# Folding the convolution's Fourier transforms round the middle of the sequence in a fused hybrid block

## What is computed

```python
b, l, d = u.shape
up = (u @ w_in + b_in).transpose(0, 2, 1)
uc = lax.conv_general_dilated(up, sf_w[:, None, :], (1,), [(KSIZE - 1, KSIZE - 1)], ...)[..., :l] + sf_b[None, :, None]
x0, x1, v = jnp.split(uc, 3, axis=1)
k = _implicit_filter(...).T
v = v * x1
n = 2 * l
y = jnp.fft.irfft(jnp.fft.rfft(v, n=n) * jnp.fft.rfft(k, n=n), n=n)[..., :l]
v = y + v * filt_bias[None, :, None]
out = (v * x0).transpose(0, 2, 1)
return out @ w_out + b_out
```

## Time and profile before

| what | value |
|---|---|
| median of 3 runs | 515.03 us (514.41 to 516.46) |
| the profiled execution's own time | 516.48 us |
| its span | 514.6 us |
| TensorE busy | 471.2 us (92%) |
| VectorE busy | 364.7 us (71%) |
| GpSimd busy | 327.0 us (64%) |
| ScalarE busy | 270.8 us (53%) |
| TensorE clock granted, mean | 0.981 |

### The profile page before, as it was taken

One profiled execution on the slowest core, in us unless ns is written; L12 is line 12 of the kernel. 1 busy time (PEld: TensorE's weight loads), 2 busy tenths in 40 slices (PEclk: granted clock), 3 DMA queues, 4 the chain that ended last, 5 costly groups with the idle time before them and its releaser, 6 DMA issues.

```text
span 514.6 us, 13024 instructions
## 1 busy us (share of the span) xinstructions
PE 471.2 (92%) x3852; PEld 367.3 (71%) x3852; DVE 364.7 (71%) x1136; ACT 270.8 (53%) x716; POOL 327.0 (64%) x446
## 2 busy tenths in 40 slices
PE   3989999999899999996899999999889999999994
PEld 1658878787665999974576676666677656999962
DVE  6688999967766656544877787878877766566635
ACT  3464444653561555544667676676765542555530
POOL 4455766648772466651798899999746771566640
PEclk9999999998999999999999999999979999999997
DMA  8999950001111233316000000000001111333229
GB/s 280 325 383 406 403 225 1 0 2 41 48 54 47 73 85 95 84 52 165 0 3 3 2 3 2 4 1 3 2 14 36 53 53 47 84 83 95 78 73 291
DMA packets 36993, 47.56 MB, mean 92 GB/s; under 512 B 4186, under 2 KB 28123, under 8 KB 36798
## 3 DMA queue, kind: packets, MB, share of 16 engines
q1 hardware_dynamic: 31648, 35.90, 21.4%
q0 software_dynamic: 4544, 9.35, 5.3%
q10 hardware_dynamic: 734, 1.50, 1.0%
HBM read 17.86 MB, written 28.87 MB: 91 GB/s over the span
## 4 chain that ended last, share of the span: by engine, by line
PE 74%; DVE 10%; ACT 8%; issue 5%; POOL 1%; DMA 0%; ACTq 0%; DVEq 0%; POOLq 0%
PE bank L783 69%; ACT silu_sh L1249 2%; PE bank L305 2%; PE bank L893 2%; DVE prod L1614 2%; ACT rows L1242 1%; ACT scores_odd L1224 1%; ACT wide L1224 1%; DVE conv_xv L1521 1%; ACT k_tok L1224 1%; PE bank L1179 1%; PE bank L795 1%; DVE residual L1620 1%; DVE prod L1791 1%; PE bank L992 1%
## 5 line engine op out<-in xcount | busy, mean ns | idle before, releaser
L660 POOL DMA_INDIRECT routed<-row_out,row_token x78 | 74.9, 960 | 66.4 <-DVE row_token L1682 49.9
L783 PE MATMUL bank<-row_in_t,row_weights 128*128 128x128 f32 x624 | 84.0, 278 | 1.9 <-issue 1.2
L783 PEld LDWEIGHTS bank<-row_in_t,row_weights 128*128 128x128 f32 x624 | 75.7, 192 | 4.2 <-issue 2.8
L651 POOL DMA_INDIRECT sorted_rows<-rows,place x64 | 62.3, 973 | 23.0 <-issue 14.3
L1290 ACT ACTIVATE row_silu<-bank 128x256 f32<-128x256 f32 x78 | 29.9, 383 | 48.2 <-PE bank L783 48.2
L1674 DVE TENSOR_SCALAR row_weights<-experts 128x512 f32 x78 | 33.9, 435 | 26.9 <-issue 23.2
L783 PE MATMUL bank<-wide,weights_sb 128*128 128x512 f32 x112 | 51.5, 597 | 0.0
L783 PE MATMUL bank<-experts,row_act 128*128 x312 | 50.1, 283 | 1.3 <-ACT row_out L1224 1.1
L1249 ACT ACTIVATE silu_sh<-bank 128x512 f32<-128x512 f32 x32 | 19.0, 594 | 60.0 <-PE bank L783 59.8
L1666 DVE TENSOR_TENSOR row_act<-row_silu,bank 128x256 f32<-128x256 f32 x78 | 32.8, 420 | 19.8 <-ACT row_silu L1290 10.9
L1224 ACT ACTIVATE wide<-bank 128x512 f32<-128x512 f32 x54 | 29.4, 592 | 30.8 <-PE bank L783 17.1
(11 more groups left out here) (194 smaller groups left out, 1092.2 us busy)
## 6 DMA issues: line engine op xcount, KB each, us to landing
sorted_rows<-zeros SPq DMA_DIRECT2D x1, 17028.0 KB, 50.6
row_in<-sorted_rows SPq DMA_DIRECT2D x78, 64.5 KB
rows<-routed SPq DMA_DIRECT2D x8, 256.0 KB, 4.9
scores_odd<-routed SPq DMA_DIRECT2D x8, 256.0 KB, 5.3
out<-residual SPq DMA_DIRECT2D x8, 256.0 KB, 3.6
routed<-row_out,row_token POOLq DMA_INDIRECT x78, 2.3
tables_sb<-tables SPq DMA_DIRECT2D x1, 1024.0 KB, 8.8
experts<-rt_gate SPq DMA_DIRECT2D x1, 1024.0 KB, 18.4
```

The costliest lines, as they stand in the source:

```text
L651: pool.indirect_dma_start(sorted_rows, bass.IndirectOffsetOnAxis(ap=place[:, t:t + 1].bitcast(U32), axis=0), rows[:, t, :], None).then_inc ...
L660: pool.indirect_dma_start(routed, bass.IndirectOffsetOnAxis(ap=row_token[:, r:r + 1].bitcast(U32), axis=0), row_out[:, r, :], None).then_i ...
L783: return pe.matmul(out_, lhsT, rhs, start=start, stop=stop, **kw)
```

## The change

The sequence is folded round its middle. Position j and position 255 - j are added into an even half and subtracted into an odd half, 128 positions each. With the transform's origin at the middle, the cosines need the even half alone and the sines the odd half, so `forward` drops the sum over s, and `inverse` makes an even half out of the cosines and an odd half out of the sines. Afterwards the sum of the two is the first half of the sequence, and their difference the second half in reversed order.

- GpSimd `value(k)`: the product as before, then a wait for it, then an addition and a subtraction of 128 x 256 elements, each of which reads half of `value_c` with a step of -1.
- TensorE `forward(k)`: 4 matmuls of 256 columns instead of 8. `inverse(k)`: 8 matmuls of 128 columns instead of 8 of 256.
- ScalarE `copy_odd(k)`: a new copy of the odd half, 256 columns, out of bank 6; it stands behind tap2 in a step. `keep(2)` and `scale_rows(1)` move ahead of copy_odd(7).
- VectorE `gate(k)`: waits for that copy, adds, subtracts (this one writes with a step of -1) into `out_c`, waits for both, and then multiplies `out_c` with `gates`.
- The buffers for it are parts of `scores_odd`, which is idle then. `gate_tap_rows`, `gate_weights` and their semaphores are declared and not used; the short convolution stays as it is. The table that is loaded for the transforms has 1024 columns as before.

```diff
+    centred = np.arange(P)[:, None] - (L - 1) / 2
+    fold_cos, fold_sin = np.cos(2 * np.pi * centred * f / NF), -np.sin(2 * np.pi * centred * f / NF)
+    fold_sin[:, 0] = -np.sin(np.pi * centred[:, 0])
+    fold = np.stack([fold_cos, fold_sin], 1)
+    c["fold_dft"] = fold
+    inv = (fold * weight).transpose(1, 2, 0)
+    c["inverse_dft"] = inv.reshape(2, FB, P, P).transpose(2, 0, 1, 3)
...
             def value(k):
                 pool.wait_ge(c_conv, 3 * k + 2)
+                pool.tensor_tensor(value_c[:], conv_xv[:, 0, :], conv_xv[:, 1, :], ALU.mult).then_inc(c_value, 1)
+                pool.wait_ge(c_value, k + 1)
                 wait(pool, c_value_turned, k)
-                pool.tensor_tensor(value_c[:], conv_xv[:, 0, :], conv_xv[:, 1, :], ALU.mult).then_inc(c_value, 1)
+                v = value_c[:].rearrange("p (b t) -> p b t", b=2)
+                folded = value_fold.rearrange("p (b h t) -> p b h t", b=2, h=2)
+                for h, op in enumerate((ALU.add, ALU.subtract)):
+                    pool.tensor_tensor(folded[:, :, h, :], v[:, :, 0:P], v[:, :, L - 1:P - 1:-1], op).then_inc(c_folded, 1)
...
             def forward(k):
                 pe.wait_ge(c_value_copied, k + 1)
                 wait(pe, c_prod, 4 * k)
-                v = value_t[:].rearrange("p (b s) d -> p s b d", s=SB)
+                if k == 0:
+                    pe.wait_ge(inverse_loaded, 16)
+                v = value_t[:].rearrange("p (b h) d -> p h b d", h=2)
                 for c in range(2):
                     for f in range(FB):
                         o = bank[4 + c][:, f * 2 * D:(f + 1) * 2 * D].rearrange("p (b d) -> p b d", b=2)
-                        for s in range(SB):
-                            last = mm(pe, o, dft[:, s, c, f * P:(f + 1) * P], v[:, s, :, :],
-                                      start=(s == 0), stop=(s == SB - 1))
+                        last = mm(pe, o, fold_dft[:, c, f * P:(f + 1) * P], v[:, c, :, :])
...
-                            last = mm(pe, bank[6][:, b * L:(b + 1) * L], y[:, c, f, b, :], inverse_dft[:, c, f, :],
-                                      start=(c == 0 and f == 0), stop=(c == 1 and f == FB - 1))
+                            last = mm(pe, bank[6][:, b * L + c * P:b * L + (c + 1) * P], y[:, c, f, b, :],
+                                      inverse_dft[:, c, f, :], start=(f == 0), stop=(f == FB - 1))
...
+            def copy_odd(k):
+                act.wait_ge(c_inverse, k + 1)
+                copy(act, out_odd, bank[6][:].rearrange("p (b h t) -> p b h t", b=2, h=2)[:, :, 1, :]).then_inc(c_odd_copied, 1)
...
             pipelined([(0, beside({6: second_apply})), (1, each(copy_value)), (1, beside({0: copy_spectrum})),
-                       (2, each(tap2)), (3, each(conv_apply)), (3, each(copy_normed)),
+                       (2, each(tap2)), (0, beside({7: third_keep})), (0, each(copy_odd)), (3, each(conv_apply)),
+                       (3, each(copy_normed)),
                        (0, beside({5: first_apply, 6: third_apply, 7: first_silu}))], PAIRS, 1, first=-1)
...
             def gate(k):
-                dve.wait_ge(c_inverse, k + 1)
+                dve.wait_ge(c_odd_copied, k + 1)
+                even = bank[6][:].rearrange("p (b h t) -> p b h t", b=2, h=2)[:, :, 0, :]
+                y = out_c.rearrange("p (b t) -> p b t", b=2)
+                dve.tensor_tensor(y[:, :, 0:P], even, out_odd, ALU.add).then_inc(c_unfolded, 1)
+                dve.tensor_tensor(y[:, :, L - 1:P - 1:-1], even, out_odd, ALU.subtract).then_inc(c_unfolded, 1)
+                dve.wait_ge(c_unfolded, 2 * (k + 1))
                 wait(dve, c_out, k)
-                dve.tensor_tensor(gated[:], bank[6][:], gates[:, bass.ds(k * PT, PT)], ALU.mult).then_inc(c_gated, 1)
+                dve.tensor_tensor(gated[:], out_c, gates[:, bass.ds(k * PT, PT)], ALU.mult).then_inc(c_gated, 1)
```

More of the change, by code:

```diff
@@ L88 @@
 TABLES, TABLES_N = packed([
-    ("identity", P), ("decay", TAU * D), ("dft", TAU * NF), ("inverse_dft", 2 * FB * L),
+    ("identity", P), ("decay", TAU * D), ("dft", TAU * NF), ("fold_dft", NF), ("inverse_dft", 2 * FB * P),
     ("causal", P), ("own_head", P), ("head_of", HEADS), ("head_in_group", IN_GROUP), ("tie_rank", E),
@@ L113, in shape_constants @@
     weight = np.where(np.arange(NF // 2) == 0, 1.0, 2.0) / NF
-    inv = (dft[:L] * weight).transpose(1, 2, 0)
-    c["inverse_dft"] = inv.reshape(2, FB, P, L).transpose(2, 0, 1, 3)
+    centred = np.arange(P)[:, None] - (L - 1) / 2
[5 more added lines that the diff above has]
+    c["inverse_dft"] = inv.reshape(2, FB, P, P).transpose(2, 0, 1, 3)
     c["identity"] = np.eye(P)
@@ L172, in hybrid_block @@
         dft = table("dft", "p (t c f) -> p t c f", t=TAU, c=2)
+        fold_dft = table("fold_dft", "p (c f) -> p c f", c=2)
         inverse_dft = table("inverse_dft", "p (c f t) -> p c f t", c=2, f=FB)
@@ L320, in hybrid_block @@
         value_c = sb("value_c", [P, PT])
+        scores_odd = sb("scores_odd", [P, 2 * HEADS * P])
+        value_fold = scores_odd[:, 0:PT]
+        out_odd = scores_odd[:, PT:PT + 2 * P].rearrange("p (b t) -> p b t", b=2)
+        out_c = scores_odd[:, 2 * PT:3 * PT]
+        gate_tap_rows = scores_odd[:, 3 * PT:3 * PT + 3 * D]
+        gate_weights = scores_odd[:, 4 * PT:4 * PT + 3 * D].rearrange("p (k d) -> p k d", k=3)
         value_t = sb("value_t", [P, PAIR, D])
@@ L336, in hybrid_block @@
         c_value = sem("c_value")
+        c_folded = sem("c_folded")
+        c_odd_copied = sem("c_odd_copied")
+        c_unfolded = sem("c_unfolded")
+        gate_taps_loaded = sem("gate_taps_loaded")
+        gate_weights_made = sem("gate_weights_made")
         c_value_turned = sem("c_value_turned")
@@ L522, in hybrid_block @@
         v_wide = sb("v_wide", [P, 3, AT, V_N])
-        scores_odd = sb("scores_odd", [P, AT * HEADS * P])
         scores = [s.rearrange("p (t h q) -> p t h q", t=AT, h=HEADS)
@@ L567, in hybrid_block @@
         at_decay, at_dft = slice(*TABLES["decay"]), slice(*TABLES["dft"])
-        at_inverse, at_rest = slice(*TABLES["inverse_dft"]), slice(TABLES["causal"][0], TABLES_N)
+        at_inverse, at_rest = slice(TABLES["fold_dft"][0], TABLES["inverse_dft"][1]), slice(TABLES["causal"][0], TABLES_N)
         conv_columns, other_columns = slice(0, WEIGHTS["w_out"][0]), slice(WEIGHTS["w_out"][0], WEIGHTS_N)
@@ L987, in turn_value @@
             def turn_value(k):
-                pe.wait_ge(c_value, k + 1)
+                pe.wait_ge(c_folded, 2 * (k + 1))
                 pe.wait_ge(ln_c.copied, min(k + 2, PAIRS))
                 for j in range(PAIR):
-                    last = pe.transpose(bank[0][:, j * P:(j + 1) * P], value_c[:, j * P:(j + 1) * P], ident)
+                    last = pe.transpose(bank[0][:, j * P:(j + 1) * P], value_fold[:, j * P:(j + 1) * P], ident)
                 last.then_inc(c_value_turned, 1)
@@ L1388, in third_apply, with third_keep, first_silu @@
                 early_apply(2)
-            def first_silu():
+            def third_keep():
                 keep(2)
                 scale_rows(1)
+            def first_silu():
                 silu_half(0, 0)
```

## The result

The changed kernel takes 518.75 us (median of 19 runs, 516.05 to 523.54); the kernel before, run beside it on the same chip, 516.64 us (19 runs, 514.41 to 517.98). The ratio is 1.0059 (95% interval 1.0042 to 1.0076): 3.0 us slower, just over the 0.5% that this kernel's measurement can tell. Forecast were 516.6 us against 515.03, so +1.6; the range of 511.8 to 521.5 holds the time. By the two medians the change costs 2.1 us and by the two means (519.46 and 516.58) 2.9; where this text says 3.0 it goes by the ratio.

A forecast was written before the change was run, and what follows sets the result against it. TensorE was taken to bound the steps, with VectorE 0.36 us behind. A balance of -0.2 us before the clock plus +1.8 for the clock gave +1.6 on 515.03: 516.6 us, range 511.8 to 521.5.

The forecast's parts named there:

- TensorE sets the step, VectorE follows 0.36 us behind: Steady steps: TensorE sets the 11.33 us; VectorE's own work is 10.97 us, leaving it 0.36 us to spare.
- TensorE's savings: Convolution in each step: forward 1.7 us shorter, inverse 1.6 us shorter, leaving TensorE 8.0 us of work.
- VectorE's +0.79: Gate in each step: addition, subtraction and product take 1.39 us instead of 0.60, so +0.79 us.
- The wait for GpSimd: Gate's product, reading two SBUF tiles, waits for GpSimd's second fold to end: +0.48 us a step.
- Steps 1 to 5: Steps 1 to 4 cost +0.91 us each, +3.6 together, step 5 +0.2; add_conv(5) moves from 101.72 to 105.5.
- The tail without the clock: Steps 6 and 7 give 4.0 us back, chiefly in inverse(7); balance over all steps -0.2 us.
- The clock: After TensorE's idle stretch in step 5, work through inverse(6) runs at half speed: +1.8 us, bounds 0 and +3.6.
- Rival 1: Gate's product does not wait for GpSimd: 513.7 us, or 511.9 if the clock holds as well; chance 0.20.
- Rival 2: GpSimd's folds are slow reading with a step of -1: 525.3 us, 521 with half the surcharge; chance 0.17.
- Rival 3: TensorE's chain at 1.2 GHz sets the steady steps: +8 us on the forecast, 524.6 us; chance 0.08.
- Rival 4: VectorE has more room than read, steps stay near 11.3 us and the tail's 4.0 are gain: 511.0 us; chance 0.10.

The follow-up runs named there:

- Experiment 5: Kernel before, with two unread additions of 256 columns on VectorE ahead of each gate; ratio 1.0017 to the kernel before.
- Experiment 6: Folds and short forward as in the change, inverse over both halves with a centred table, gate as before; ratio 0.9933 to the kernel before.
- experiment 8: Short inverse, copy_odd and three-operation gate as in the change, value and forward as before; ratio 0.9988 to the kernel before.
- experiment 2: Changed kernel with unread 512-column multiplications filling TensorE's gaps through the steps, steps 5 and 6 included; ratio 1.0004 to the kernel before.
- experiment 3: Changed kernel with unread 512-column multiplications only in TensorE's gaps of steps 5 (four) and 6 (two); ratio 0.9998 to the kernel before.
- experiment 9: As experiment 3, but one filler in step 6 and silu's table load with scale_rows(0) ahead of copy_odd(6) on ScalarE; ratio 1.0084 to the kernel before.

## Why the prediction was right, and what was mis-sized

**TensorE sets the step, VectorE follows 0.36 us behind: right.** Experiment 5 measured 0.38. Experiment 6 took TensorE's work away, and the step fell to VectorE's 10.95 to 11.10 us and no further.

**TensorE's savings: right.** Forward went from 3.62 to 1.89 us in the timeline and inverse from 3.62 to 1.95, so 1.73 and 1.67 less; forecast were 1.7 and 1.6.

**VectorE's +0.79: right.** From the first of the three instructions to the product 53.70 - 52.92 = 0.78 us, and experiment 8's step of 11.75 has it alone.

**The wait for GpSimd: right in kind, smaller than said.** +0.36 us (1.05 for 0.69) instead of +0.48. The stretch was right: the product was ready at 53.70 (said 53.84) and the folds ended at 54.21 (said 54.32), 0.51 us. But the product ends 0.54 us behind the folds, not its full 0.69: about 0.15 of it passes during the wait. The row that the prediction read shows the same, as the edge correction of 0.15 us ended 0.02 behind GpSimd's addition; the prediction added the whole wait. With 0.78 + 0.36 and the wait for TensorE gone, VectorE's 10.97 becomes 12.11; forecast was 12.2. The Trainium skill (SBUF — State Buffer, on who interferes with whom) says that of a VectorE operation with two SBUF inputs and a GpSimd operation that reads SBUF, the one that issues second blocks until the first is done. The traces agree beside GpSimd's operations of 256 and 512 columns: 1.05, 0.34 and 1.13 us where 0.69, 0.15 and 0.19 are usual, and 0.68 us where the gate reads a bank in the middle of the folds. They do not agree beside GpSimd's power of 4 columns (`rstd<-rstd,neg_half`): in the kernel before it runs from 92.23 to 93.25, and an edge correction starts at 92.31 and takes 0.13 us. For such an operation the measurement decides: VectorE was not stopped for the whole of it.

**Steps 1 to 5: right.** add_conv(5) is at 105.27, forecast 105.5. Two of the steps were 12.31 us; there the first edge correction came 0.14 us later behind the statistics, in steps that follow a project at the lower clock.

**The tail without the clock: right.** The balance before the clock was put at -0.2 us. Experiments 2 and 3, with the clock held, measure 1.0004 and 0.9998, so +0.2 and -0.1 us, each known to 0.6 to 0.8. Both sides of the balance were too large, though, and their errors cancel: in experiment 3 add_conv(5) is 3.0 us later than before (said 3.8) and project_out(7) 0.4 earlier (said 0.2), so the tail gave back 3.4 (said 4.0). That much of the hit is luck. The table load is at 108.6 to 108.8 there (said 109.2), project_out(7) at 122.2 to 122.4 (said 122.6).

**The clock: the term that was mis-sized.** The place was right: step 5's stand of 3.77 us (said about 4), then project_out, two turns, gate(0) and inverse(6) at half speed. Taken was +1.8, with bounds 0 and +3.6. Measured is 1.0059 - 0.9998 = 0.0061, so +3.2 us by the ratios, known to about 1.2, and near the upper bound: I had assumed that the clock would be back for inverse(6), and in the trace it was not (3.72 us). The figure is an average over two groups of executions, and no trace shows how the clock goes in the larger one, which loses about 1 us. In the profiled execution it is 522.0 - 516.5 = 5.5 us against experiment 3's, beyond the bound, because there the clock falls a second time: gate(2) and inverse(7) ran at 0.5, 1.87 and 3.74 us, and gate(7) with its copy_odd came right behind them. The prediction took inverse(7) for off the path. At full speed it is: in experiment 3 its copy_odd ends at 119.59, and VectorE comes to the gate at 120.82.

**The total** lies 2.1 us above the forecast of 516.6. Of these 1.6 are the reference: the three runs of before that were known had a median of 515.03, nineteen have 516.64. Of the slowdown, 3.0 us were measured by the ratio and 1.6 forecast; the 1.4 between them are the clock's. The range, 511.8 to 521.5, holds the time, but its ends are not quite the sums that it names, 511.9 and 521.

**The rivals.** Rival 1 (no wait for GpSimd) fell with the 1.05. Rival 2 (backward is slow) fell with 0.41 us for both directions and 1.41 us for two folds. Rival 3 (the clock sets the step) fell in its strong form: experiment 3 has stretches at 0.50 inside steps of 12.11 us. Its cause was real, and its place was the tail. Against it stood that "a slower TensorE idles less, which brings the clock back": in the changed kernel the clock did come back within each step, and behind the fall in step 1 TensorE waited only 0.33 and 0.80 us in step 2, where it did not fall. Rival 4 fell with the step.

## What to carry to other kernels

When a change takes work from the engine that leads by little, price its second half by the engine behind it. Here the forward's half alone was a gain (no operation more on VectorE, 0.7%, with its first gap filled 1.2%), and with the inverse's half beside it nothing of that was left, even with the clock held (0.9998). And where TensorE gets idle time, look for the place where its next matmuls are on the path again: gaps in the steady steps were free, those of 3.8 us in step 5 and 2.2 us in step 6 together cost 3.2 us, and six useless multiplications bought it back.

## What the runs showed of the hardware that I had not expected

- Reading or writing with a step of -1 cost nothing: 0.41 us for 256 columns on VectorE in either direction, 1.41 us for the two folds on GpSimd.
- The granted clock fell to 0.50 behind gaps of 1.5 and 2.3 us in one step, but not in each step: in experiment 3 it fell in steps 1 and 3 and held in step 2, with the same work and the same length of 12.11 us. The waits were not the same. In steps 1 and 3 TensorE waited 1.60 and 2.18, and 1.70 and 2.09 us; in step 2, where it came late from the slow stretch before, 0.48 and 1.66. In these traces a slow stretch took up idle time, and the step behind it had less. But the wait alone does not decide it: in experiment 8 TensorE waited 1.9 us ahead of project_out in each of steps 1 to 4, and the clock fell in step 4 alone. In experiment 2, with the gaps filled, it never fell in the steps. The Trainium skill (TensorE: Matmul & The Clock Gate, on the clock gate) has the gate follow how busy the array has recently been; the traces agree in that all falls shown here stand behind idle time.
- A gap need not be long for it: in the kernel before, inverse(7) took 5.39 us behind two stretches of matmuls on 8 columns with a gap of 0.7 us before the second. But it is not certain there: with one multiplication of 512 columns in that gap inverse(7) took 3.70 us, and in two of the four traces without one it took 3.70 as well (experiments 5 and 6).
- A VectorE operation of 0.19 us can take 1.13 us beside GpSimd. It pays what is left of GpSimd's operation: 1.13 us when it starts 0.18 us into the sum (experiment 9), 0.36 when it starts 0.96 into it (experiment 3).
